# Window attention layer: the step that copies the row maxima into the query rows, at another place in each stage's order

## The reference, cut to what matters

```
q = apply_rope(proj(Wq, bq)) * Dh ** (-0.5)        # 16 heads of width 16
k = apply_rope(proj(Wk, bk)); v = proj(Wv, bv)
scores = einsum('bhqd,bhkd->bhqk', q, k)
scores = where((rel > 0) | (rel < -128), -inf, scores)     # rel = key - query
probs = softmax(scores)
out = einsum('bhqk,bhkd->bhqd', probs, v) @ Wo.T + bo
x = layernorm(x + out)
```

## Time and profile before

| | before |
|---|---|
| median of 3 runs | 2969.61 us (2962.3 to 2972.91) |
| the profiled execution | 2967.14 us |
| its span, first to last instruction | 2965.0 us |
| mean granted TensorE clock | 0.903 |
| TensorE matmuls busy | 2357.0 us, 79% |
| VectorE busy | 1519.0 us, 51% |
| ScalarE busy | 895.3 us, 30% |
| GpSimd busy | 600.1 us, 20% |

### The profile page before, as it was taken

How to read it: one execution, slowest core, us unless ns; L and a number is a source line. 1 busy time by engine, 2 the same in 40 slices (tenths; PEclk the granted TensorE clock), 3 DMA queues, 4 the chain that set the end, 5 groups by cost and what they waited for, 6 DMA issues and landing times. The chain is left out here.

```text
span 2965.0 us, 44749 instructions
## 1 busy us (share of the span) xinstructions
PE 2357.0 (79%) x18544; PEld 1454.3 (49%) x18544; DVE 1519.0 (51%) x2671; ACT 895.3 (30%) x1265; POOL 600.1 (20%) x340
## 2 busy tenths in 40 slices
PE   3888888999898885856567389898288888898896
PEld 1344544444444443735455245665155555555553
DVE  2445444445454543454645334655566566765662
ACT  0233332333333333423333122221032343333332
POOL 3121111112221101010101033333211122112212
PEclk7899999999999998878888799999588999999998
DMA  6455555444544534566566510110442453245230
GB/s 141 86 101 101 109 103 112 100 94 102 106 108 94 99 60 143 187 199 239 183 232 210 175 59 29 57 57 1 147 118 73 138 145 89 85 138 147 66 91 31
DMA packets 235288, 337.57 MB, mean 114 GB/s; under 512 B 14816, under 2 KB 172880, under 8 KB 234832
## 3 DMA queue, kind: packets, MB, share of 16 engines
q1 hardware_dynamic: 232272, 334.07, 42.4%
q10 hardware_dynamic: 2816, 0.65, 0.1%
HBM read 206.10 MB, written 127.93 MB: 113 GB/s over the span
## 5 line engine op out<-in xcount | busy, mean ns | idle before, releaser
L444 ACT ACTIVATE l0a_probs<-l0a_slot 128x1024 f32<-128x1024 f32 (+1 forms) x256 | 247.4, 970 | 419.5 <-PE l0a_slot L606 419.3
L1620 ACT ACTIVATE l1f_probs<-l1f_slot 128x1024 f32<-128x1024 f32 x240 | 241.0, 1022 | 428.1 <-PE l1f_slot L1793 293.3
L501 DVE TENSOR_REDUCE l0a_rowmax<-l0a_slot 128x4 f32<-128x1024 f32 (+1 forms) x256 | 293.4, 1156 | 126.6 <-PE l0a_slot L606 123.7
L1683 DVE TENSOR_REDUCE l1f_rowmax<-l1f_slot 128x1 f32<-128x1024 f32 x240 | 287.7, 1219 | 100.5 <-PE l1f_slot L1779 100.3
L601 PE MATMUL l0a_slot<-l0a_maskT,l0a_ident 128*128 128x512 bf16 (+1 forms) x512 | 161.6, 400 | 73.7 <-issue 67.9
L1793 PE MATMUL l1f_slot<-l1f_Qs,l1f_Ks 128*128 128x256 f32 x960 | 185.5, 320 | 40.8 <-DVE l1f_rowmax L1683 16.6
L1793 PEld LDWEIGHTS l1f_slot<-l1f_Qs,l1f_Ks 128*128 128x128 f32 x960 | 142.7, 202 | 110.9 <-DVE l1f_rowmax L1683 29.9
L1779 PE MATMUL l1f_slot<-l1f_Ks,l1f_Qs 96*128 96x512 f32 x480 | 172.4, 453 | 29.3 <-DMA l1f_Qs<-kq_rows 16.5
L601 PE MATMUL l0a_slot<-l0a_mask,l0a_ident 128*128 128x512 bf16 (+1 forms) x512 | 150.3, 376 | 25.7 <-issue 23.4
L404 POOL TENSOR_TENSOR l0a_turned<-l0a_turned 128x512 f32<-128x512 f32 x32 | 40.7, 1273 | 634.8 <-DVE l0a_turned L487 634.8
L1738 PE MATMUL l1f_os<-l1f_probs,l1f_V 128*32 128x256 f32 x1920 | 165.6, 397 | 2.0 <-ACT l1f_probs L1620 1.1
(11 more groups left out here) (186 smaller groups left out, 4018.7 us busy)
## 6 DMA issues: line engine op xcount, KB each, us to landing
expert_outputs<-l0f_inter SPq DMA_DIRECT2D x64, 512.0 KB, 2.6
l0f_wide<-expert_outputs SPq DMA_DIRECT2D x32, 1024.0 KB, 9.6
l0a_Qs<-qk_rows SPq DMA_DIRECT2D x96, 256.0 KB, 7.9
l0a_Ks<-qk_rows SPq DMA_DIRECT2D x96, 256.0 KB, 15.0
l1f_Ks<-kq_rows SPq DMA_DIRECT2D x48, 512.0 KB, 6.9
l0f_f<-in_dram SPq DMA_DIRECT2D x10, 2048.0 KB, 15.4
qk_rows<-l0a_hi SPq DMA_DIRECT2D x32, 512.0 KB, 2.8
qk_rows<-l0a_lo SPq DMA_DIRECT2D x32, 512.0 KB, 4.2
```

Source lines behind the costliest of these rows:

```text
L444: exp_ready.by(act.activation(probs[:, t % 2, HG * g:HG * g + HG, 0:reach, :], s[:, :, 0:reach, :], ACT.Exp, scale=SCALE))
L501: max_ready.by(dve.reduce_max(rowmax[:, t, :, 2 * g:2 * g + 2], s[:, :, :, first:2 * P], AX))
L1620: exp_done.by(act.activation(probs[:, half, u - FIRST[i], :], s[:, :], ACT.Exp, scale=SCALE))
L1683: max_done.by(dve.reduce_max(rowmax[:, 2 * u + t:2 * u + t + 1], s[:, :], AX))
```

## The change

In each stage, `place` is taken from the end and made the second entry of the stream that has `maxT` and `back`. That stream has three entries instead of two, so its keys go from 1/4 and 3/4 to 1/6, 1/2 and 5/6.

```
@@ -257,8 +257,7 @@
         steps += [(0, "oT", i)]
-        steps += merged([(ot, "tr", NHG * tt + g) for g in range(NHG)], [(on, "maxT", tn), (0, "back", i)], front[i])
-        steps += [(on, "place", tn)]
+        steps += merged([(ot, "tr", NHG * tt + g) for g in range(NHG)], [(on, "maxT", tn), (on, "place", tn), (0, "back", i)], front[i])
         if i == 2:
```

## The result

| | median, us | lowest to highest | profiled span, us | granted clock, mean |
|---|---|---|---|---|
| before (here 3 runs, later more) | 2969.6 | 2962.3 to 2972.9 | 2965.0 | 0.903 |
| changed, 4 runs | 2881.6 | 2875.8 to 2884.5 | 2879.5 | 0.922 |

The changed kernel takes 0.970 of the time (95% interval 0.967 to 0.974), 86 to 88 us less. The direction was right, the size was not.

What follows compares the result with a forecast made beforehand. TensorE was taken to set the pace, idling 4.5 us a block ahead of stage 0 for stage 3's `place`. The terms -46 - 18 + 12 + 2 = -50 us gave 2917, 2920 on the median's scale, range 2886 to 2984.

Steps and rivals of the forecast that it cites:

- Term 1: Stage 3's `place` goes out earlier, shortening the wait ahead of stage 0: -46 us, bounds -68 and 0.
- the fixed delay: Bound for stage 3's `place`: 11.6 us from issue to landing whatever stands ahead, so every wait goes, 67.9 us.
- the landing at the turn of the DMA rate: Bound for stage 3's `place`: it lands when the stack is through, at about 517.5, as before; gain 0.
- Term 2: TensorE's mask matmuls behind the wait mostly keep their clock instead of running at half speed: -18 us, bounds -24 and 0.
- Term 3: In stage 0 the early issue delays ScalarE's third exponential, 0.85 us in each of 14 blocks: +12 us, bounds +5 and +13.
- Term 4: In stage 3 the issue delays `l0a_aoT` and so the `v` projection by some 0.3 us: +2 us, bounds 0 and 4.
- Term 5: In stages 1 and 2 the earlier issue holds up nothing that is needed, and no one waited for their DMAs: zero.
- the whole wait goes: Rival: all waits ahead of stage 0 and all clock loss vanish, -76 us, 2894 on the median's scale; chance 0.32.
- `place` stays behind the stack: Rival: stage 3's `place` lands at the stack's end + 1.5 us, waits stay, stage 0 pays 12 us: 2982; chance 0.20.

Runs made afterwards that it cites:

- b3: Kernel before plus probe DMAs of 4 KB on ScalarE's queue at other points in stages 3 and 0, landings marked by GpSimd; one profiled run, 2961.7 us.
- a2: Against the changed kernel, `place` is early in stage 3 alone and at the end of the other stages; 2875.8 us, ratio 0.969.
- c2: Against the changed kernel, `place` is early in stages 0 and 3 only, at the end in stages 1 and 2; 2881.6 us.
- a1: The changed kernel once more, run beside its variants on one chip; 2886.8 us, ratio 0.973.
- a3: Against the changed kernel, `place` is early in stages 0, 1 and 2 but at the end in stage 3; 2971.4 us, ratio 1.001.
- b4: b3 with the stack cut into 24 DMAs of 128 KB instead of 12 of 256 KB, same bytes; one profiled run, 2955.3 us.
- c1: Against the kernel before, `place` of stage 3 alone is moved, one `tr` slot later than in a2; 2889.7 us, ratio 0.973.
- c3: a2 again, run beside c1 and c2 on one chip; 2878.7 us.
- a4: Against the kernel before, `place` of stage 3 moves straight behind `maxT`, one `tr` slot earlier than a2, VectorE's order kept; 2903.3 us, ratio 0.979.

## Why the prediction was wrong, point by point

- **What bounds the kernel** was read rightly: one wait a block, for `place` of stage 3, in front of stage 0. It went, and nothing came in its stead.
- **Term 1, the wait, -46 us: here the forecast failed.** The step was "No row decides it; I take the middle, 3.2 us", with a depth between 1.4 and 2.3 MB. The 15 waits went from 67.2 to 2.6 us in the profiled run, a term of -65 (the 67.9 of the forecast had the 0.68 of the earlier trace rows in them, so that the mean wait was 4.5 us all the same). The depth lay at the lower end: `place` is served 1.21 to 1.32 MB behind its issue in the kernel before and 1.29 to 1.36 MB in the changed one. Of the two bounds the fixed delay was nearly right (b3: 11 to 12 us at the points of issue in stage 3; 12.5 to 13.8 us in the three blocks of the changed kernel that still wait, where 11.6 had been assumed), and the landing at the turn of the DMA rate was a coincidence of one point of issue. A middle between two mechanisms is the time of neither: landing 3.2 us earlier would have been a delay of 14.7 us, which no block of the changed kernel shows.
- **Term 2, the clock, -18 us, bounds -24 and 0.** Against the floor of 6.74 us the kernel before loses 8.19 - 6.74 = 1.45 us a block, -22 us in 15 blocks. The mechanism and the 1.6 us were right; the 0.4 us a block that was held back belonged to the waits that did not stay. The bound was too tight: in the trace of b2, the same kernel but for two swapped instructions, the yardstick is 9.26 us, a loss of 2.5 us a block. The pair behind the wait is also a poor witness of the clock. In the block of 651.62 it takes 0.61 us, and yet that block loses 2.2 us, because the clock falls a moment later.
- **Term 3, stage 0, +12 us, bounds +5 and +13.** Right in kind (a2, c2), 0.53 us a block instead of 0.85, 7.4 us in all. The issue was taken to begin with the `xT` copy. It begins 0.33 us earlier (424.64 against 424.97), since `place` doesn't wait for the slot that the copy reads.
- **Term 4, stage 3, +2 us.** From the output projection to the `v` projection TensorE took 16.46 us on average before and 16.63 after: 0.17 x 14 = +2.4.
- **Term 5, stages 1 and 2.** Zero, as c2 against a1 shows in the traces.
- **The sum** with the measured terms is -64.6 - 21.8 + 7.4 + 2.4 = -76.6 us, against -81.1 at the layer's end: 4.5 us of the layer aren't assigned. Another 4.4 us lie in the layers behind it, where the same code takes 1796 us before, 1792 after and 1789 in a3, so these traces show no cause for them.
- **The rival that came true**, the whole wait goes, had -76 us and 2894. The time is 12 us below that. The stages 0 and 3 cost 6 us less than in its sum, but the waits and the clock brought 6 us less too. What is left is the 4.5 us of the layer without a term, the 4.4 us in the later layers, and the 2.5 us that the forecast added for the median, which is at the profiled execution in the changed kernel (2881.6 and 2881.5). The range ended too soon: 2886 left this rival a margin of 8 us. The rule of the Trainium skill on turns between queues spoke for this rival, and deserved more weight than the coincidence that spoke against it.
- **`place` stays behind the stack** would have needed the landing to keep to the turn. The probe of b3 shown above lands 5.4 us ahead of `place`, with 0.9 MB of the stack overtaken.

## What to carry to other kernels

When a small DMA lands just as a large transfer ends, don't conclude that it waits for it: put a probe at another point of issue and see whether the delay or the landing stays, and count what the other queue moves between issue and first packet. If that amount is fixed, all that counts is the distance between issue and need (here about 13 us), and more distance buys nothing. A DMA issue belongs behind an instruction that its engine is then busy with, not ahead of one that another engine waits for: the same two DMAs cost 0.2 us a block behind an exponential in stage 3, 0.5 us in stage 0, and 1.4 us one slot earlier, where VectorE's copy was late as well. The best kernel of this study moves `place` in stage 3 alone, 2876 and 2879 us, a ratio of 0.969 and 0.970.

## What the runs showed of the hardware

- A DMA of 4 KB on ScalarE's queue, issued 6 to 9.4 us into a sequence of 256 KB DMAs on SyncE's, lands 10.9 to 12.4 us after its issue (b3). Its packets go when SyncE's queue has moved another 1.28 to 1.35 MB, ahead of up to 0.9 MB that was issued before it. In b4, where less than that is ahead of it, they go when all but 18 to 61 of the pieces ahead have gone, and it lands after 5.4 to 9.4 us. With no stack under way the whole of `place` takes 2.5 us.
- The clock fell also after shorter waits than those of the kernel before. In c1 it did after one of 1.53 us; the first pair still runs at full speed, and the next groups at 1.2 GHz, as the stretches of 2 us from 233 on show (the columns of the earlier trace rows):

```profile
233.62 0.59 PE L602 MATMUL l0a_slot<-l0a_maskT,l0a_ident 128*128 128x512 bf16 x2 [1.53 <-issue]
235.76 1.04 PE L602 MATMUL l0a_slot<-l0a_maskT,l0a_ident 128*128 128x512 bf16 x2 [0.20 <-ACT l0a_probs L445]
```
```profile
233.00:235.00 2.00, 1.38 (x10) 0.85 (x11) 0.35 (x1) 0.31 (x1) 0.00 (x0) 0.99 1.03 150
235.00:237.00 2.00, 1.80 (x8) 0.47 (x7) 0.28 (x1) 1.19 (x2) 0.00 (x0) 0.50 1.06 357
237.00:239.00 2.00, 2.00 (x10) 1.23 (x10) 0.00 (x0) 1.42 (x2) 0.00 (x0) 0.50 0.35 120
```

  That block's yardstick is 9.17 us. In the block of 485.00 a wait of 1.07 us leaves it at 6.72.
- What a fall of the clock costs varies from execution to execution of much the same code, 1.45 us a block in one trace and 2.5 in another, while without the waits (a2, c3, a4) the yardstick is 6.72 to 6.75 us in every block. A wait that is taken away takes its scatter with it.
